# First-half scan decays in PSUM with one bank for value products, and half of a convolution on GpSimd

## The reference

```
xn = layernorm(x)
x  = x + attention(xn) + experts(xn)       # layer 0: 16 heads over the full width, causal; 8 experts, two used
xn = layernorm(x)
x  = x + mamba(xn) + local_transformer(xn) # layer 1
```

```
xc    = silu(conv(xin, conv_w) + conv_b)         # causal, 15 taps, each channel by itself
delta = softplus(dt_low @ W_dt + b_dt);  A = -exp(A_log)
for t: h = h * exp(delta_t * A) + delta_t * B_t * x_t     # h is [ED, N]
       y_t = sum over N of h * C_t
y = (y + xc * D_param) * silu(z)
```

## Time and profile before

| | us |
|---|---|
| median of 3 runs | 2651.05 (2650.94 to 2651.4) |
| the profiled execution | 2648.06 |
| its span, first to last instruction | 2646.3 |
| granted clock of PE, mean of the span | 0.978 of full |

### The profile page before, as it was taken

How to read it: one execution, slowest core, us unless ns; L and a number is a source line. 1 busy time by engine, 2 the same in 40 slices (tenths; PEclk the granted TensorE clock), 3 DMA queues, 4 the chain that set the end, 5 groups by cost and what they waited for, 6 DMA issues and landing times. The chain is left out here.

```text
span 2646.3 us, 67497 instructions
## 1 busy us (share of the span) xinstructions
PE 2376.9 (90%) x26742; PEld 1412.5 (53%) x26742; DVE 2351.0 (89%) x2535; ACT 1850.7 (70%) x4093; POOL 1887.6 (71%) x1739
## 2 busy tenths in 40 slices
PE   7999999797877787989989999999999999999997
PEld 4444433333222234666656666666666666666665
DVE  6778879979999997899858899999998999899994
ACT  4666554555565554777768888888888888888884
POOL 2441242247877866777668899989998999899991
PEclk9999999999999998999989999999999999999999
DMA  3000000012222211120111112111211122111101
GB/s 106 9 10 10 9 7 9 23 19 46 49 50 52 49 33 35 52 57 14 46 49 32 36 30 64 40 30 38 64 44 26 36 66 41 25 35 37 31 22 39
DMA packets 171111, 97.22 MB, mean 37 GB/s; under 512 B 97155, under 2 KB 167791, under 8 KB 169263
## 3 DMA queue, kind: packets, MB, share of 16 engines
q1 hardware_dynamic: 170799, 92.91, 15.3%
HBM read 66.91 MB, written 7.08 MB: 28 GB/s over the span
## 5 line engine op out<-in xcount | busy, mean ns | idle before, releaser
L603 PE MATMUL ps<-xnT,qp 128*128 128x512 f32 (+3 forms) x1280 | 571.2, 565 | 28.8 <-ACT prob L828 28.1
L828 ACT ACTIVATE prob<-ps,mneg,shift 128x1024 f32<-128x1024 f32 (+7 forms) x384 | 366.0, 954 | 304.2 <-DVE mneg L723 302.2
L1901 DVE TENSOR_TENSOR area<-ps,tab 128x2048 f32<-128x2048 f32 x192 | 430.4, 2283 | 64.8 <-ACT area L1687 40.1
L723 DVE TENSOR_REDUCE mneg<-ps 128x1 f32<-128x1024 f32 (+7 forms) x384 | 339.4, 884 | 71.4 <-PE ps L603 70.9
L1418 PE MATMUL ps<-wqk,area 128*128 128x512 f32 x768 | 359.4, 610 | 28.4 <-DVE area L1967 23.7
L2088 POOL TENSOR_TENSOR area<-area,rn 128x1024 f32<-128x1024 f32 x192 | 370.5, 1950 | 7.5
L731 DVE STREAM_TRANSPOSE area<-prob 128x1024 f32<-128x1024 f32 (+7 forms) x384 | 350.8, 914 | 25.2 <-ACT prob L828 23.6
L1508 PEld LDWEIGHTS ps<-wvo,area 128*128 128x128 f32 x3072 | 352.1, 192 | 26.9 <-issue 20.9
L1508 PE MATMUL ps<-wvo,area 128*128 128x128 f32 x3072 | 358.8, 275 | 3.3 <-ACT area L1736 3.3
L603 PEld LDWEIGHTS ps<-xnT,qp 128*128 128x128 f32 x1280 | 221.4, 197 | 223.7 <-issue 170.2
L1729 ACT ACTIVATE ps<-ps,nmxl 128x64 f32<-128x64 f32 x1536 | 321.3, 343 | 5.7 <-DVE nmxl L1881 5.5
(11 more groups left out here) (273 smaller groups left out, 4366.3 us busy)
## 6 DMA issues: line engine op xcount, KB each, us to landing
xe<-bc_scratch SPq DMA_DIRECT2D x128, 128.0 KB, 3.7
area<-bc_scratch SPq DMA_DIRECT2D x128, 128.0 KB, 4.0
staged<-values_scratch SPq DMA_DIRECT2D x192, 32.0 KB, 1.9
wqk<-lwqk_dram SPq DMA_DIRECT2D x6, 1024.0 KB, 6.5
xp<-xc SPq DMA_DIRECT2D x96, 48.0 KB, 2.7
xc<-xs SPq DMA_DIRECT2D x96, 32.0 KB
wvT<-lwvT_dram SPq DMA_DIRECT2D x6, 512.0 KB, 7.8
...
```

The costliest lines, as they stand in the source:

```text
L603: mm = E.matmul(ps[:, r + o // 512, 0:w], k.qp[:, group % 2, i * P:(i + 1) * P], k.xnT[:, k0 + o:k0 + o + w], start=o // 512 != masked, st ...
L723: V.tensor_reduce(k.mneg[:, U:U + 1], of, X_AXIS, ALU.max, negate=True).then_inc(s("top"), 1)
L828: A.activation(k.prob[:, U % 2, 0:nk], ps[:, r:r + 2, :].rearrange("p a b -> p (a b)")[:, 0:nk], ACT.Exp, bias=k.mneg[:, U:U + 1], scale=k ...
L1901: V.tensor_tensor(k.rot[:, n % 2, w, :, :].rearrange("p c (h d) -> p c h d", d=DH), bcast(heads(what, n), 1, 2), bcast(k.tab[:, n % FRAME, ...
```

## The change

1. `k.dc`, the decays, are one place of 2 x 256 in PSUM bank 7 instead of two places in SBUF. `unit_decay(u)` therefore waits for scan u-1, and it moves from the even piece to the odd one, behind `unit_state`.
2. Bank 7 is made free: all value products but the last batch's go to bank 6 (`value_bank`). The first product of batch b therefore waits for `oL` of batch b-1 (before: of b-2). `shares` leaves slots 1 and 2 of a batch without products.
3. In SBUF the place of the decays is taken by `k.hc`, the product with C. POOL's product no longer overwrites `k.hx`, and its wait for `state` moves to the inputs two units later.
4. POOL makes the second channel half of the convolution, a tap in each step 25 to 39: a TENSOR_SCALAR into a scratch tile and a TENSOR_TENSOR that adds it. DVE keeps the first half, 15 taps over steps 22 to 44. The tail copy moves from step 38 to 41. The second SiLU waits for both.

The second stage keeps two places in SBUF (`k.decay_places = 2`, `k.hc = k.hx`).

```diff
--- before.py
+++ after.py
@@ -354,8 +354,8 @@
     "dve": ["rec", "sa", "stats1", "mv1", "var1", "stats2", "mv2", "var2"]
-    + [f"conv{a}" for a in range(ET)],
+    + ["conv0"],
@@ -405,7 +405,12 @@
 def shares(b):
 
-    return (4, 4, 4, 4, 4, 4, 8) if is_square(b) else (0, 4, 4, 4, 4, 8, 8)
+    return (0, 0, 8, 4, 4, 8, 8) if is_square(b) else (0, 0, 4, 4, 8, 8, 8)
+
+
+def value_bank(b):
+
+    return 7 if b == NB - 1 else 6
@@ -461,10 +466,10 @@
 def unit_decay(k, u):
     A, s = k.ac, k.sem
-    if u >= 2:
-        A.wait_ge(s("scanned"), u - 1)
+    if u >= k.decay_places:
+        A.wait_ge(s("scanned"), u + 1 - k.decay_places)
     for a in range(ET):
-        ins = A.activation(k.dc[:, u % 2, a, :], k.dl(u // NS)[:, a, :], ACT.Exp, scale=k.alog[:, a, u % NS:u % NS + 1])
+        ins = A.activation(k.dc[:, u % k.decay_places, a, :], k.dl(u // NS)[:, a, :], ACT.Exp, scale=k.alog[:, a, u % NS:u % NS + 1])
@@ -485,7 +490,7 @@
-        ins = V.tensor_tensor_scan(h, k.dc[:, b, a, :], h, k.last[:, i, a:a + 1] if c else 0.0, ALU.mult, ALU.add)
+        ins = V.tensor_tensor_scan(h, k.dc[:, u % k.decay_places, a, :], h, k.last[:, i, a:a + 1] if c else 0.0, ALU.mult, ALU.add)
@@ -501,9 +506,9 @@
-    G.tensor_tensor(k.hx[:, b, :, :], k.hx[:, b, :, :], bcast(k.bc[:, 1, b, :], 1, ET), ALU.mult).then_inc(s("h_c"), 1)
+    G.tensor_tensor(k.hc[:, b, :, :], k.hx[:, b, :, :], bcast(k.bc[:, 1, b, :], 1, ET), ALU.mult).then_inc(s("h_c"), 1)
     G.wait_ge(s("h_c"), u + 1)
-    G.tensor_tensor(y, y, k.hx[:, b, :, :], ALU.add).then_inc(s("y_sum"), 1)
+    G.tensor_tensor(y, y, k.hc[:, b, :, :], ALU.add).then_inc(s("y_sum"), 1)
@@ -660,8 +665,8 @@
-            if b >= 2:
-                E.wait_ge(s("oL"), b - 1)
+            if 0 < b < NB - 1:
+                E.wait_ge(s("oL"), b)
@@ -669,7 +674,7 @@
-            mm = E.matmul(ps[WIN * c:WIN * (c + 1), 6 + x, WIN * i0:WIN * NTH], k.vb[:, x, NTH * c + f // 4, :], of, start=f < 4, stop=f >= HALF - 4,
+            mm = E.matmul(ps[WIN * c:WIN * (c + 1), value_bank(b), WIN * i0:WIN * NTH], k.vb[:, x, NTH * c + f // 4, :], of, start=f < 4, stop=f >= HALF - 4,
@@ -780,8 +785,8 @@
-            for x in range(ET * KC * i // n, ET * KC * (i + 1) // n):
-                conv(*divmod(x, KC))
+            for t in range(KC * i // n, KC * (i + 1) // n):
+                conv(0, t)
@@ -888,7 +893,8 @@
-            A.wait_ge(s("half_dve"), at["dve"]["conv1"])
+            A.wait_ge(s("half_dve"), at["dve"]["conv0"])
+            A.wait_ge(s("half_pool"), at["pool"]["conv1"])
             A.activation(k.mu, k.mu, ACT.Silu).then_inc(s("half_act"), ev.up("silu_u"))
@@ -925,11 +931,13 @@
+        elif U >= FIRST:
+            j = step_of(U - 1)
+            if scanned_in(j - 1) is not None:
+                unit_state(k, scanned_in(j - 1))
             if scanned_in(j) is not None:
                 A.wait_ge(s("half_pool"), at["pool"]["du"])
                 unit_decay(k, scanned_in(j))
-        elif U >= FIRST and scanned_in(step_of(U - 1) - 1) is not None:
-            unit_state(k, scanned_in(step_of(U - 1) - 1))
@@ -1010,7 +1018,21 @@
+    def conv(t):
+
+        x, y, part = k.mxp[:, 1, :], k.mu[:, 1, :], k.work[:, 0, :]
+        if t == 0:
+            G.wait_ge(s("half_act"), at["act"]["in1"])
+            G.tensor_scalar(y, x[:, 0:TH], k.taps[:, 1, 0:1], k.cols[:, 7:8], ALU.mult, ALU.add).then_inc(s("half_pool"), ev.up("tap0"))
+            return
+        G.wait_ge(s("half_pool"), ev.n)
+        G.tensor_scalar(part, x[:, t:t + TH], k.taps[:, 1, t:t + 1], None, ALU.mult).then_inc(s("g"), k.g.up())
+        G.wait_ge(s("g"), k.g.n)
+        G.tensor_tensor(y, y, part, ALU.add).then_inc(s("half_pool"), ev.up(f"tap{t}" if t < KC - 1 else "conv1"))
+
     def branch(j):
+        if 25 <= j < 25 + KC:
+            conv(j - 25)
@@ -1051,7 +1073,6 @@
     def outputs(u):
-        G.wait_ge(s("state"), u + 1)
         unit_outputs(k, u)
@@ -1067,6 +1088,8 @@
             if scanned_in(j) is not None:
+                if scanned_in(j) >= 2:
+                    G.wait_ge(s("state"), scanned_in(j) - 1)
                 unit_inputs(k, scanned_in(j))
@@ -2241,7 +2264,8 @@
-            k.dc, k.hx = (k.work[:, i, :].rearrange("p (b a t) -> p b a t", b=2, a=ET) for i in range(2))
+            k.decay_places, k.dc = 1, k.ps[:, 7, :].rearrange("p (b a t) -> p b a t", b=1, a=ET)
+            k.hx, k.hc = (k.work[:, i, :].rearrange("p (b a t) -> p b a t", b=2, a=ET) for i in range(2))
```

More of the change, by code:

```diff
@@ L356 @@
     "dve": ["rec", "sa", "stats1", "mv1", "var1", "stats2", "mv2", "var2"]
-    + [f"conv{a}" for a in range(ET)],
-    "pool": ["acc0", "centred1", "pow1", "xn", "centred2", "pow2", "hat", "rest1", "rest2", "pad", "first", "tail", "y", "relu0", "delta0",
+    + ["conv0"],
+    "pool": ["acc0", "centred1", "pow1", "xn", "centred2", "pow2", "hat", "rest1", "rest2", "pad", "first"] + [f"tap{t}" for t in range(KC - 1)] + ["conv1", "tail", "y", "relu0", "delta0",
              "relu1", "delta1", "du"] + [x for i in range(2) for x in (f"gate{2 * i}", f"gate{2 * i + 1}", f"mo{i}")],
@@ L554, in attention_sp @@
         elif j == 46:
-            S.wait_ge(s("half_dve"), at["dve"]["conv1"])
+            S.wait_ge(s("half_dve"), at["dve"]["conv0"])
             S.wait_ge(s("half_pool"), at["pool"]["tail"])
@@ L681, in gather @@
         for q in range(4):
-            mm = E.matmul(ps[WIN * q:WIN * (q + 1), 6 + b % 2, 256:256 + DV0 * NTH], k.pick[:], of[:, q, :, :], start=True, stop=True, skip_group_check=True)
+            mm = E.matmul(ps[WIN * q:WIN * (q + 1), value_bank(b), 256:256 + DV0 * NTH], k.pick[:], of[:, q, :, :], start=True, stop=True, skip_group_check=True)
         mm.then_inc(s("pick_mm"), 1)
@@ L737, in turn_values @@
             V.wait_ge(s("pick_mm"), b - 1)
-        V.transpose(k.oT[:, b % 2, :], ps[:, 6 + b % 2, 0:WIN * NTH]).then_inc(s("ot"), 1)
+        V.transpose(k.oT[:, b % 2, :], ps[:, value_bank(b), 0:WIN * NTH]).then_inc(s("ot"), 1)
     def moments(i, src):
@@ L845, in gathered @@
         A.wait_ge(s("pick_mm"), b + 1)
-        A.activation(to.rearrange("p i v -> p (i v)"), ps[:, 6 + b % 2, 256:256 + DV0 * NTH], ACT.Copy).then_inc(s("oL"), 1)
+        A.activation(to.rearrange("p i v -> p (i v)"), ps[:, value_bank(b), 256:256 + DV0 * NTH], ACT.Copy).then_inc(s("oL"), 1)
     def visit(what, i, z):
@@ L1031, in branch @@
             G.tensor_copy(k.xs[:, 1:NTH + 1, :], k.xn[:, 0:NTH, :]).then_inc(s("half_pool"), ev.up("first"))
-        elif j == 38:
+        elif j == 41:
             G.wait_ge(s("half_act"), at["act"]["in1"])
@@ L1982, in scan @@
             h = k.hx[:, b, a, :]
-            ins = V.tensor_tensor_scan(h, k.dc[:, b, a, :], h, k.last[:, i, a:a + 1], ALU.mult, ALU.add)
+            ins = V.tensor_tensor_scan(h, k.dc[:, u % k.decay_places, a, :], h, k.last[:, i, a:a + 1], ALU.mult, ALU.add)
         ins.then_inc(s("scanned"), 1)
@@ L2292, in build @@
             k.dl, k.du, k.ym = (lambda c, x=x: x for x in (dl, du, ym))
+            k.decay_places = 2
             k.dc, k.hx = (k.acc[:, 8 * i:8 * i + 8, :].rearrange("p (b a t) d -> p b a (t d)", b=2, a=ET) for i in range(2))
+            k.hc = k.hx
             k.accf = k.wqk[0][:, 0:T].rearrange("p (t d) -> p t d", d=P)
```

## The result

| | us |
|---|---|
| before, median of 4 runs | 2650.99 (2644.24 to 2651.4) |
| after, median of 4 runs | 2581.59 (2579.47 to 2583.71) |
| ratio, 95% interval | 0.9744 (0.9725 to 0.9763) |
| after, the profiled execution; its span | 2579.93; 2578.1 |

The change makes the kernel 2.6% faster. It was predicted at 2595 with a range of 2578 to 2620.

The account below looks back on a forecast made before the run. DVE was taken as the limit in the convolution and the scan. From 2648.06 us profiled, 52 for the scan and 4 for the convolution left 2592; the median, 3.0 higher, was forecast at 2595, range 2578 to 2620.

Parts of the forecast that it names:

- The scan's limit and the hold-up: Scan: DVE limits; its two-SBUF-operand scans and POOL hold each other up; decays in PSUM save 58.2 us.
- rival 6: Scan: the hold-up stays with PSUM decays, only the convolution gains; 2647 us, no change; 4%.
- Scan stretch 52 us: Scan, 378.7 us before: 58.2 us saved, less 6 charged for DVE's new waits, gives 52.
- Rival 3: Scan: PE or POOL limits the stretch, which lasts 346 us, 33 less instead of 52; 2614 us; 16%.
- ACT's decays behind the scan: Scan: ACT's decays, waiting for the previous scan, fit before the next one; cost 0.
- One bank: Products in the batches: with one bank and a later slot, ACT's copy is done 1.0 us ahead; cost 0.
- Rival 5: Products in 47 batches: ACT's copy is late for the one bank and PE stands; slower, 2689 us; 3%.
- The convolution's 4 us: Convolution: 7.5 us gained end to end, less 2.5 given back by PE and 1 for the second SiLU.
- Rival 4: Convolution: POOL's one-input half doesn't hold DVE; 23 us saved, some 15 passed by PE; 2584 us; 10%.
- POOL's time: Convolution: POOL's taps take 78 to 81 us, DVE's taps hold it 12 x 1.2; done at 516 to 519.
- rival 2: Convolution: POOL's half ends 12 to 17 us later and the second SiLU waits; about 2610 us; 12%.
- forecast of 2591: Convolution: by the one-input line-rate rule a POOL tap takes 3.5 us, DVE waits some 4 us less; time 2591.

Follow-up runs that it names:

- experiment 3: Changed kernel with the decays in one place in SBUF, the product with C in place and POOL's wait for the state as before: 2634.61 us.
- experiment 4: Changed kernel, decays still in PSUM, but the product with C in place and POOL's wait for the state as before: 2578.09 us.
- Experiment 7: Changed kernel with products one slot earlier, the first again in slot 2, still one bank: 2598.74 us.
- experiment 10: Changed kernel with a second operator in POOL's scaling and seven of DVE's taps also on POOL, summed at step 41: 2580.85 us.
- experiment 9: Changed kernel with a second operator, the addition of 0.0, in POOL's TENSOR_SCALAR of a tap: 2585.05 us.

## Why the prediction was right, point by point

- **The scan's limit and the hold-up: right.** Forecast 58.2 us off the scans; measured 150.4 - 91.4 = 59.0. Scans lie within 0.65 to 0.75 us (those without a carried state, at 0.67, were not told apart in the forecast's 0.72). Experiments 3 and 4 show that the memory of the operand decides, so rival 6 falls. The page "SBUF — State Buffer" of the Trainium skill, section "Who interferes with whom", states the same for DVE: one SBUF input doesn't contend with GpSimd, two do, when GpSimd's instruction reads SBUF.
- **Scan stretch 52 us: the direction right, the term of 6 us for new waits mis-sized.** The stretch gave 57.9. DVE idles 5.4 us there, but 3.6 of that were there before (378.70 - 375.11), so only 1.8 were new. A pair of batches lasts 320.8 / 8 = 40.1 us, where 40.8 was forecast. Rival 3 (PE or POOL limits) didn't come: PE is busy 87% and POOL 88%, near the forecast's 92 and 90%, and yet DVE idles little. What it does wait for is POOL's inputs, in 5.0 of the 5.4 us, three times of four with a `vb` ahead of them. The prediction read the 3.4 us before the change as waits for ACT's decays. There too, at the first of its three places, the decays had ended 0.56 us before the scan of 698.85 and POOL's inputs only 0.09 us before it.
- **ACT's decays behind the scan, nothing: right.** At the three scans that waited without a named releaser, the decays had been ready for 2.2 us.
- **One bank, nothing: right.** Margin 1.15 us for the 1.0 worked out, batches 1 to 21 0.8 us shorter, no wait of PE's products for ACT's copy to 1000 us. Experiment 7 shows what stood behind it: 13.9 us over those batches. Rival 5 falls.
- **The convolution's 4 us: the step that failed is "a tap that comes up at random waits for half of what POOL runs".** It counted all of POOL's instructions as holding. Measured, DVE's 14 taps cost 22.6 us instead of 33, and the stretch gave 11.7. Rival 4 (10%) named this mechanism: 23 us saved on DVE, 15 passed on, 2584. Its figure lies 2.4 us from the result, in part by luck: the scan gave 5.9 us more than it counted and the convolution 3.3 less. It was right for the later two thirds of each one-operator TENSOR_SCALAR and wrong for the first 0.93 us. Of the 16.3 us that taps lost within the stretch (36.7 + 0.8 before, 21.2 after), 11.7 passed. PE at 90.66 of 98.30 us is the next limit: DVE idles 2.2 us more, for it. The rest, 2.4 us, was never there to save: DVE's records overlap (they sum to 120.2 us before, with 109.79 busy, and to 104.0 after, with 95.93), and with 13 instructions fewer 2.3 us of overlap went too. DVE's other instructions are the same, 82.7 us before and 82.8 after.
- **POOL's time: the end was right for a reason partly wrong.** It started 2 us earlier, and tap 0 took 1.20 us, below the lower bound of 2.84: the nearest row, a TENSOR_SCALAR of another line, didn't bound a form with two operators. POOL's other taps came to 78.2 us, of which only 5.5 are DVE's doing (14 x 5.19 = 72.7 without it), not 12 x 1.2. So `conv1` was done at 506.42 instead of 516 to 519, but the shorter convolution had drawn the SiLUs forward as well, and it came 0.9 us ahead of its SiLU, within the 2 us forecast, so rival 2 (12%) was closer than the result shows, and experiment 10 walks into it.
- **The rule that one-input operations run at roughly line rate** ("GPSIMD Engine Reference" of the Trainium skill, section 4.1) does not fit the form used here, 2.84 us, and fits the form with two operators, 1.12 against 1.04 for a copy. Where the forecast of 2591 that was drawn from it rested on shorter waits of DVE, experiment 9 speaks against it: the faster form made them longer.

The sum, term by term: -52 became -57.9, -4 became -11.7, batches 27 to 30 cost 2.2 that nobody had charged, and the rest made -0.8. Both terms were too small, so the result lies in the lower part of the range and the figure is 13 us high. Some 0.6 of the 2.2 us is the mark at batch 31 that moved. Most of the rest goes with PE's clock: the stretch lasts 88.9 us with a granted clock of 0.94 in the changed kernel and in experiment 3, and 86.8 with 0.96 in experiment 4. PE's busy time there differs by as much (79.8 us against 77.7), 1.55 of it in the scores at 537.25 shown above. Why the clock fell there, and not in experiment 4, is open.
